# Causal grouped-query attention of a decoder's first layer, rewritten

## The chip, the cores and the metric

One core of one Trainium2 chip runs the whole program: four decoder layers over 1024 tokens of width 128. The metric is the device time of the program in microseconds (us). A core has five engines that work side by side and meet only at semaphores: TensorE (PE, matrix products, with its weight loads PEld), VectorE (DVE), ScalarE (ACT), GpSimd (POOL) and SyncE (SP, transfers). TensorE's clock has two levels, 1.2 and 2.4 GHz; a profile gives the granted clock as 0.50 or 1.00.

## The reference

The change lies in the first sublayer, x = x + attention(layernorm(x)):

```python
q = rms_norm(bitlinear(x, Wq).reshape(8, 128, 16, 8)...)   # in effect 1024 tokens, 16 heads of width 8
k = rms_norm(bitlinear(x, Wk)...)                          # 4 key and value heads
v = bitlinear(x, Wv)...
q, k = apply_rotary(q, cos, sin), apply_rotary(k, cos, sin)
q = q * q_gain[None, :, None, None]
k, v = jnp.repeat(k, 4, axis=1), jnp.repeat(v, 4, axis=1)
...                                                        # causal softmax(q k' / sqrt(8)) v
return bitlinear(y, Wp)
```

There are 1024 tokens, so eight tiles of 128. Each of 16 heads has a causal 1024 by 1024 matrix of scores; four heads share a key head. `bitlinear` rounds weights to three values and activations to 8 bits. The other eleven sublayers (cross-attentions, feed-forward layers, a scan and so on) are not touched.

## The kernel before

`ternary_attention` (L2095) normalises x, builds the quantised weights, projects to q, keys and values, turns them by the rotary table (L2216 to L2234), repeats keys and values for all 16 heads (L2236 to L2241), calls `attend` (L1021), and then projects and adds the result (L2243 to L2263). All this runs in blocks, one after the other, with a barrier of all engines at the end of each.

Before the weights are summed, VectorE writes `mask8` (L2135 to L2141): for each tile of queries a row of bytes over all 1024 keys, 251 where the key is later than the query and 0 elsewhere.

`attend` goes through the heads in eight pairs; a head of the pair is a = 0 or 1. Scores are exact to float32 by splitting queries and keys into three bf16 parts each and laying six products of parts below one another: `kstack` and `qstack` have 64 columns a head, of which 48 hold parts, one a constant, and three the shift. TensorE turns both stacks (L1191, L1197), and VectorE copies them to `kturned` and `qturned` (L1322, L1324), where head 0 has rows 0 to 51 and head 1 rows 64 to 115. GpSimd builds the next pair's stacks during the pair before (`stacks`, L1154).

For every pair, twice the scores are formed:
- Pieces ("chunk" items): TensorE multiplies a tile of queries with up to 512 keys (L1205), first all 12 of head 0 and then all 12 of head 1, and VectorE takes the row maxima under the byte mask with one fused instruction (L1334). From the maxima it computes the shift of each query, splits it into three parts and writes these into `qstack` (`place_shift`, L1351 to L1368). Then the queries are turned a second time.
- Scores: for a tile of keys t and a head a, TensorE forms the scores of all queries from 128 t on, in two products of up to 512 columns (L1225), and adds the mask of the diagonal block by a product of `mask8` with a diagonal matrix (L1229). ScalarE takes the exponential of up to 1024 columns at once (L1303). TensorE multiplies it, in float32, with the values and a column of ones (`weigh`, L1247): four products, for two heads and two halves of the queries, that lie on separate quarters of the array's columns, nine columns wide each.

Pieces of the next pair are put between the scores of this one, three places a tile (`some_items`), and go through a ring of three PSUM banks; scores have four banks and the weighed values one. At a pair's end ScalarE copies the four sums (L1309), TensorE turns them, and VectorE divides by the ones' sum and writes the output (L1340, L1342). The order is the same on each engine, and each waits for counts.

The kernel's own cross-attentions (`cross`, L1639, with the order from `programme`, L1610) already work by halves of the queries: pieces of both heads at once into two banks (L1762) with one reduction for both (L1885), scores of 512 columns (L1800), exponentials (L1855), weighings of two tiles of keys at once (L1816) and a fold of the sums (L1827).

Of the kernel before, what the change touches and what calls it, by code (L numbers as in the profile page):

```python
# [12 lines left out]
P = 128  # L13
T = 1024
NT = T // P
D = 128
H = 16
HD = D // H
# [1002 lines left out]
def attend(k, tiles, q, keys, values, out, key_mask=None, mask8=None, causal=False):  # L1021

    nc = k.nc
    n_keys = tiles * P
    kgroups = [range(a, min(a + 8, tiles)) for a in range(0, tiles, 8)]
    chunks = [(a, min(a + BANK, n_keys)) for a in range(0, n_keys, BANK)]
    NC, NG = len(chunks), len(kgroups)  # L1040

    def span(t, c):

        lo, hi = chunks[c]
        return lo, min(hi, (t + 1) * P) if causal else hi

    def first_query(t):

        return t * P if causal else 0


    prepare = ([("keys", g) for g in range(NG)] + [("queries", 0)] +
               [("chunk", a, t, c) for a in range(2) for t in range(NT) for c in range(NC) if span(t, c)[1] > span(t, c)[0]] +
               [("queries", 1)])
    G = len(prepare)
    FILL = 3 * (tiles - (4 if tiles > 2 * NT else 1))
    STEPS = 6 + (4 if mask8 is not None else 0)

    def before(p, a, b):

        if isinstance(p, int) and p == 0:
            return a
        return 2 * a + (p - 1) * (a + b)

    def items_of(p, par):

        first, last = isinstance(p, int) and p == 0, isinstance(p, int) and p == PAIRS - 1
        items = [] if last else [(item, p + 1, 1 - par) for item in prepare]
        return items if first else items[:NG] + [(("sums",), p - 1, 1 - par)] + items[NG:]

    def sums_place(p):
        return 0 if isinstance(p, int) and p == PAIRS - 1 else NG

    def phases(eng, phase, straight=False):

        phase(0, 0)
        if straight:
            for p in range(1, PAIRS):  # L1080
                phase(p, p % 2)
            return
        with eng.Fori(0, PAIRS // 2 - 1) as i:
            phase(2 * i + 1, 1)
            phase(2 * i + 2, 0)
        phase(PAIRS - 1, 1)

    with Stage(nc) as s:
        kstack = s.sb("kstack", [P, tiles, 2, SLOT], BF16)
        qstack = s.sb("qstack", [P, 2, NT, 2, SLOT], BF16)  # L1090
        kturned = s.sb("kturned", [P, 2, n_keys], BF16)
        qturned = s.sb("qturned", [P, 2, T], BF16)
        vstack = s.sb("vstack", [P, 2, tiles, 2, HD + 1])
        left = s.sb("left", [P, max(tiles, NT), 2, HD])
        probs = s.sb("probs", [P, 4, T])
        maxima = s.sb("maxima", [P, 2 * NT, NC])
        shift = s.sb("shift", [P, 2 * NT])
        shift_left = s.sb("shift_left", [P, 2 * NT])
        empty = s.sb("empty", [P, 2, 2 * NT])
        sums = s.sb("sums", [P, BANK])  # L1100
        inverse = s.sb("inverse", [P, 2 * NT])
        junk = s.sb("junk", [P, 4, BANK], BF16)
        cleared = s.sem("cleared")
        first_order = s.sem("first_order")
        no_maxima = s.sem("no_maxima")
        pool_order = s.sem("pool_order")
        stacks_ready = s.sem("stacks_ready")
        values_ready = s.sem("values_ready")
        ring_filled = s.sem("ring_filled")
        ring_free = s.sem("ring_free")  # L1110
        dve_order = s.sem("dve_order")
        shift_ready = s.sem("shift_ready")
        scores_filled = s.sem("scores_filled")
        probs_ready = s.sem("probs_ready")
        unit_done = s.sem("unit_done")
        sums_taken = s.sem("sums_taken")
        block = s.block()

        def ring(j):
            return 5 + j % 3  # L1120

        def score_buffer(n):
            return k.ps[:, 2 * (n % 2):2 * (n % 2) + 2, :].rearrange("p a b -> p (a b)")

        N_CLEAR = 6 + (key_mask is not None)

        def split(e, o, src, stack, first, second, third, last_step=None):

            rest = left[:, 0:src.shape[1]]

            def slot(i):
                return stack[:, :, :, i * HD:(i + 1) * HD]
            o.step(e.tensor_copy(slot(first[0]), src))
            o.step(e.tensor_tensor(rest, src, slot(first[0]), ALU.subtract))
            o.step(e.tensor_copy(slot(second[0]), rest))
            o.step(e.tensor_tensor(rest, rest, slot(second[0]), ALU.subtract))
            o.step(e.tensor_copy(slot(third[0]), rest))
            copies = [(slot(i), slot(part[0])) for part in (first, second, third) for i in part[1:]]
            for dst, src2 in copies[:-1]:
                o.step(e.tensor_copy(dst, src2))  # L1140
            return copies[-1]

        per_pair = 2 * 8 - 1

        def stacks(eng, e, o, pp, par):

            src = keys[:, :, 16 * pp:16 * pp + 16].rearrange("p t (a d) -> p t a d", a=2)
            dst, last = split(e, o, src, kstack, (0, 1, 2), (3, 4), (5,))
            o.step(e.tensor_copy(dst, last))
            src = q[:, :, 16 * pp:16 * pp + 16].rearrange("p t (a d) -> p t a d", a=2)  # L1150
            dst, last = split(e, o, src, qstack[:, par], (0, 3, 5), (1, 4), (2,))
            e.tensor_copy(dst, last).then_inc(stacks_ready, 1)
            eng.wait_ge(stacks_ready, pp + 1)


        @block.gpsimd
        def _(pool):
            pool.wait_ge(cleared, N_CLEAR)

            def value_stack(pp, par):  # L1160
                src = values[:, :, 16 * pp:16 * pp + 16].rearrange("p t (a d) -> p t a d", a=2)
                nc.gpsimd.tensor_copy(vstack[:, par, :, :, 0:HD], src).then_inc(values_ready, 1)

            def stacks_of(pp):
                stacks(pool, nc.gpsimd, InOrder(pool, pool_order, (pp - 1) * per_pair), pp, pp % 2)

            value_stack(0, 0)
            value_stack(1, 1)
            pool.wait_ge(ring_filled, NG)
            pool.wait_ge(stacks_ready, 1)  # L1170
            stacks_of(1)
            for pp in range(2, PAIRS):

                pool.wait_ge(ring_filled, before(pp - 2, G, 1) + NG)
                stacks_of(pp)
                pool.wait_ge(unit_done, (pp - 1) * tiles)
                value_stack(pp, pp % 2)


        @block.tensor  # L1180
        def _(pe):
# [2541 lines left out]
```

## Time and profile before

| | us |
|---|---|
| median of 3 runs | 6687.87 (6675.5 to 6690.6) |
| the profiled execution | 6692.29 |
| its span, first to last instruction | 6690.5 |
| `attend`, first clear to last output | 73.1 to 407.0 |
| TensorE busy in the span | 4558.4 (68%) |
| VectorE, ScalarE, GpSimd busy | 3719.9, 2700.4, 753.0 |

Mean granted clock of TensorE over the span: 0.79. A row of the windows gives a stretch, its length, each engine's busy time with the number of instructions, the granted clock, the share of time in which the DMA engines worked, and GB/s. A row of the timeline gives start, duration, engine, line, operation, output<-inputs, shape out<-in and how many instructions it merges; for a matmul the shape begins with rows*columns of its weights.

### The profile page before, as it was taken

How to read it: one execution, taken by the hardware profiler on the slowest of the kernel's cores; microseconds unless marked ns; L12 is line 12 of the kernel's file. 1: busy time of each engine (PE TensorE's matmuls, PEld its weight loads, DVE VectorE, ACT ScalarE, POOL GpSimd, SP SyncE). 2: the span in 40 equal slices, each digit the busy share in tenths (PEclk: the TensorE clock that was granted, in tenths of full speed). 3: DMA queues.
4: the chain of work that ended last, by engine and by line, in shares of the span. 5: the costliest groups of instructions: out<-in, count | busy, mean ns of one | idle time of the engine just before them, and what ended most of it. 6: DMA issues, size and time to landing. Idle time of an engine off the chain costs nothing. (4 is left out here: it accounts for less than half of the span.)

```text
span 6690.5 us, 85981 instructions
## 1 busy us (share of the span) xinstructions
PE 4558.4 (68%) x32752; PEld 1806.1 (27%) x32752; DVE 3719.9 (56%) x8303; ACT 2700.4 (40%) x4930; POOL 753.0 (11%) x949
## 2 busy tenths in 40 slices
PE   5866999533799999999737999997764040524326
PEld 1233444322122222222431222222443030313225
DVE  5444666555877777774349989894343030412314
ACT  1322666233366666666214777787101010101103
POOL 1100000001000000000020000000002627161350
PEclk5567999767799999999867999999865555555557
DMA  0020000033000000000030010000040000000000
GB/s 12 0 48 18 10 14 9 14 146 106 1 11 11 11 11 10 3 10 1 6 96 1 11 22 11 11 11 10 24 130 5 11 4 12 2 11 4 7 10 3
DMA packets 105806, 142.42 MB, mean 21 GB/s; under 512 B 41998, under 2 KB 82029, under 8 KB 102512
## 3 DMA queue, kind: packets, MB, share of 16 engines
q1 hardware_dynamic: 65742, 118.14, 6.7%
q0 software_dynamic: 20480, 10.53, 1.0%
q10 hardware_dynamic: 19178, 8.34, 0.5%
q8 instruction: 255, 4.18, 0.3%
q14 instruction: 151, 1.24, 0.1%
HBM read 103.79 MB, written 33.14 MB: 20 GB/s over the span
## 5 line engine op out<-in xcount | busy, mean ns | idle before, releaser
L1855 ACT ACTIVATE probs<-ps 128x512 f32<-128x512 f32 x3264 | 1734.3, 598 | 762.8 <-PE ps L1800 762.6
L1890 DVE CUSTOM_DVE_ANT_0 junk<-ps,mask 128x512 bf16<-128x512 f32 (+1 forms) x1664 | 1049.2, 678 | 380.1 <-PE ps L1762 364.0
L1885 DVE TENSOR_REDUCE maxima<-ps 128x2 f32<-128x1024 f32 (+1 forms) x832 | 956.6, 1200 | 128.2 <-PE ps L1762 121.9
L1816 PE MATMUL ps<-probs,vstack 128*9 128x512 f32 x6528 | 872.6, 596 | 0.4 <-ACT probs L1855 0.4
L1800 PE MATMUL ps<-qturned,kturned 52*128 52x512 bf16 x3264 | 793.4, 386 | 83.5 <-ACT probs L1855 64.5
L1762 PE MATMUL ps<-kturned,qturned 49*128 49x512 bf16 (+1 forms) x3328 | 704.6, 392 | 139.4 <-DMA kturned<-ends_row 56.3
L3189 POOL DMA_INDIRECT line<-table,index x640 | 609.5, 952 | 1204.9 <-DVE index L3460 580.5
L1793 PE MATMUL ps<-maskT,lower 128*128 128x512 fp8e5 x1632 | 562.5, 387 | 63.6 <-ACT probs L1855 15.1
L1800 PEld LDWEIGHTS ps<-qturned,kturned 52*128 52x128 bf16 x3264 | 196.2, 93 | 791.8 <-ACT probs L1855 462.1
L1762 PEld LDWEIGHTS ps<-kturned,qturned 49*128 49x128 bf16 x3328 | 166.3, 95 | 520.9 <-issue 234.5
L3513 DVE SCALAR_TENSOR_TENSOR x_sb<-ps,gate,x_sb 128x128 f32<-128x128 f32 x64 | 22.5, 351 | 499.4 <-DMA rows<-in_ctx 349.7
L1793 PEld LDWEIGHTS ps<-maskT,lower 128*128 128x128 bf16 x1632 | 123.5, 96 | 599.1 <-ACT probs L1855 434.0
L3289 PE MATMUL ps<-hash_b,ones 1*128 1x128 f32 x128 | 37.3, 378 | 345.5 <-issue 293.5
L3346 ACT ACTIVATE hash_hid<-ps,hash_b 128x128 f32<-128x128 f32 x256 | 73.1, 369 | 475.0 <-DMA rows<-in_ctx 318.8
L2775 PE MATMUL ps<-plane,bands 32*32 32x512 f32 x6720 | 249.6, 608 | 17.6 <-DVE top L2927 17.6
L2873 ACT COPY powerT<-ps 128x512 f32<-128x512 f32 x280 | 164.2, 586 | 203.5 <-PE ps L2789 203.4
L2917 DVE SCALAR_TENSOR_TENSOR plane<-keep,ps 128x1024 f32<-128x1024 uint8 x144 | 175.7, 1220 | 102.7 <-PE ps L2757 102.3
L2865 ACT ACTIVATE power<-power,bias 128x512 f32<-128x512 f32 x280 | 202.5, 724 | 56.1 <-DVE bias L2935 56.1
L1544 POOL MEMSET vall<- 128x816 f32 x2 | 3.1, 1567 | 1872.2 <-POOLq L66 1872.2
L2789 PE MATMUL ps<-ident,power 128*128 128x128 f32 x1120 | 183.0, 286 | 32.4 <-ACT powerT L2873 31.4
L2927 DVE CUSTOM_DVE_ANT_0 power<-ps,lose 128x512 f32<-128x512 f32 x280 | 176.9, 687 | 41.5 <-PE ps L2775 41.5
L3319 ACT ACTIVATE dev_h<-red 128x16 f32<-128x16 f32 x16 | 3.4, 215 | 423.4 <-issue 261.3
(731 smaller groups left out, 5569.0 us busy)
## 6 DMA issues: line engine op xcount, KB each, us to landing
raw<-in_mask_BxSxS_if SPq DMA_DIRECT2D x8, 3202.0 KB, 13.2
kturned<-keys_parts SPq DMA_DIRECT2D x192, 102.0 KB
table<-lines SPq DMA_DIRECT2D x51, 256.0 KB, 2.3
line<-table,index POOLq DMA_INDIRECT x640
keys_parts<-parts SPq DMA_DIRECT2D x24, 384.0 KB, 2.5
values_heads<-vall SPq DMA_DIRECT2D x2, 3672.0 KB, 10.7
vstack<-values_heads SPq DMA_DIRECT2D x16, 459.0 KB, 16.8
lose<-in_mask_SxS_bc SPq DMA_DIRECT2D x32, 128.0 KB
```

The source lines that it names most:

```text
L1762: last = nc.tensor.matmul(ring(e)[:, a * BANK:a * BANK + hi - lo], qturned[rows, par, t * P:(t + 1) * P], kturned[rows, par, lo:hi], start ...
L1793: nc.tensor.matmul(k.ps[:, (v + j) % 3, :], k.lower[:], maskT[:, t, b * BANK:(b + 1) * BANK], start=True, stop=False, skip_group_check=True)
L1800: nc.tensor.matmul(k.ps[:, v % 3, :], kturned[rows, par, t * P:(t + 1) * P], qturned[rows, par, b * BANK:(b + 1) * BANK], start=maskT is N ...
L1816: last = nc.tensor.matmul(k.ps[at:at + HD + 1, 3, :], vstack[:, p % 2, a, t, :], probs[:, (h * KT + t) % slots, a, :], start=(t < 2), stop ...
L1855: nc.scalar.activation(probs[:, u % slots, a, :], k.ps[:, (2 * u + a) % 3, :], ACT.Exp, scale=(1.0 if maskT is None else 1.0 / STEP8)).the ...
L1885: nc.vector.tensor_reduce(dst, ring(e).rearrange("p (a n) -> p a n", a=2)[:, :, 0:hi - lo], AX.X, ALU.max).then_inc(ring_free[at % 2], 1)
L1890: nc.vector.tensor_tensor_reduce(junk[:, at % 2, a * BANK:a * BANK + hi - lo], ring(e)[:, a * BANK:a * BANK + hi - lo], mask8[:, 4 * b + m ...
L2775: last = nc.tensor.matmul(k.ps[32 * j:32 * j + 32, i, :], bands[32 * i:32 * i + 32, 4 * g + j, c, :], plane[32 * i:32 * i + 32, u % 2, j, ...
L2789: last = nc.tensor.transpose(k.ps[:, 6, m * P:(m + 1) * P], power[:, u % 2, i, (4 * b + m) * P:(4 * b + m + 1) * P], k.ident[:])
L2865: nc.scalar.activation(part, part, ACT.Exp, bias=bias[:, u % 2, 1, i:i + 1], scale=1.0 / TINY).then_inc(powers, 1)
L2927: nc.vector.tensor_tensor_reduce(power[:, u % 2, i, b * BANK:(b + 1) * BANK], k.ps[:, i, :], lose[:, win % 2, i, b * BANK:(b + 1) * BANK], ...
L3189: nc.gpsimd.indirect_dma_start(line[:, t % 4, j, :], None, lines_of, bass.IndirectOffsetOnAxis(ap=index[:, t, j:j + 1], axis=0)).then_inc( ...
```

## The change

`attend` is replaced by `causal_attend`, with an order of its own:
- The stacks of all 8 pairs (queries) and all 4 key heads are built at once at the start, on VectorE and ScalarE (queries) and GpSimd (keys and values), and kept. Keys and values are no longer repeated. The keys of a key head are turned once for its two pairs.
- The work goes by halves of the queries: 16 halves h (pair h // 2, b = h % 2), with 4 tiles of keys for b = 0 and 8 for b = 1. One exponential covers one head's 512 queries at most; scores have three PSUM banks, the weighed values one, and the ring two pairs of banks.
- A piece holds both heads: two products into two banks. VectorE takes both maxima with one reduction, without a mask. Instead TensorE adds a constant to the diagonal block by a further product per head. Bytes and `mask8` go; `hidden` is one 128 by 128 block.
- The pieces of half h + 2 are spread over the units of half h; the shift of half h + 1 stands second in that queue. `weigh` takes two tiles of keys for both heads.

```diff
+def causal_programme(lag):
+    def chunks_of(h):
+        return [("piece", h, m, c) for m in range(4) for c in range(h % 2 + 1)]
+    queue = []
+    for h in range(HALVES):
+        mine = chunks_of(h + 2) if h + 2 < HALVES else []
+        if h % 2 == 0 and h + 2 < HALVES:
+            p = (h + 2) // 2
+            mine = ([("keys", p // 2)] if p % 2 == 0 else []) + [("queries", p)] + mine
+        if h and h + 1 < HALVES:
+            mine.insert(1, ("shifted", h + 1))
+        queue.append(mine)
+    queue[0] = chunks_of(1) + [queue[0][0], ("shifted", 1)] + queue[0][1:]
+    out = [("keys", 0), ("queries", 0)] + chunks_of(0) + [("shifted", 0)]
...
+            late.setdefault(u + lag, []).append(("weigh", h, t // 2))
...
+        cut = [-(-len(queue[h]) * (3 * t + j) // (3 * n)) for j in range(4)]
+        out += [("score", h, t, 0)] + queue[h][cut[0]:cut[1]] + [("score", h, t, 1)] + queue[h][cut[1]:cut[2]]
+        out += late.pop(u, []) + queue[h][cut[2]:cut[3]]
...
+        def _(pool):
+            o.step(nc.gpsimd.tensor_copy(k_slot(0, 0), src))
...
+            nc.gpsimd.tensor_copy(kstack[:, :, :, 1, 0:half].rearrange("p t v r -> p (t v) r"),
+                                  kstack[:, :, :, 0, 0:half].rearrange("p t v r -> p (t v) r")).then_inc(keys_ready, 1)
...
+            def piece(e):
...
+                for a in range(2):
+                    rows = slice(a * SLOT, a * SLOT + SHIFT)
+                    last = nc.tensor.matmul(ring(e)[:, a * BANK:a * BANK + n], qturned[rows, p, t * P:(t + 1) * P],
+                                            kturned[rows, p // 2, c * BANK:c * BANK + n], start=True, stop=not at_end,
+                                            skip_group_check=True)
+                if at_end:
+                    for a in range(2):
+                        last = nc.tensor.matmul(ring(e)[:, a * BANK + n - P:a * BANK + n], k.lower[:], hidden[:], start=False, stop=True,
+                                                skip_group_check=True)
...
+            def score(e):
...
+                masked = [m for m in range(4) if m == t - 4 * b or (b, t, m) == (0, 1, 0)]
+                last = nc.tensor.matmul(k.ps[:, v % 3, q0:], kturned[rows, p // 2, t * P:(t + 1) * P],
+                                        qturned[rows, p, b * BANK + q0:(b + 1) * BANK], start=True, stop=not masked,
+                                        skip_group_check=True)
...
+            def weigh(e):
...
+                for t in (2 * i, 2 * i + 1):
+                    q0 = first_column(b, t)
+                    for a in range(2):
+                        at = 32 * (2 * a + t % 2)
+                        last = nc.tensor.matmul(k.ps[at:at + HD + 1, 3, q0:], vstack[:, p // 2, t, :],
+                                                probs[:, unit_at[h, t] % slots, a, q0:],
+                                                start=(t < 2), stop=(t >= n - 2), skip_group_check=True)
...
+                nc.vector.tensor_reduce(dst, ring(e).rearrange("p (a n) -> p a n", a=2)[:, :, 0:n], AX.X,
+                                        ALU.max).then_inc(ring_free[ring_at[e] % 2], 1)
```

`first_column(b, t)` is 128 times the tiles by which t lies inside the half, and 0 for the second tile of the first half, whose first block is masked whole.

## Rows read from the trace of the kernel before

**Rows 1.** windows of 138 to 403 and 3580 to 3660 us, all engines
```profile
core 0: us, PE busy (x) PEld busy (x) DVE busy (x) ACT busy (x) POOL busy (x), PEclk, DMA share, GB/s
138.00:378.00 240.00, 210.89 (x840) 53.28 (x838) 106.46 (x384) 76.53 (x122) 27.99 (x86) 0.50 0.00 0
...
378.00:403.00 25.00, 23.39 (x86) 5.10 (x86) 0.71 (x3) 11.56 (x20) 0.00 (x0) 0.50 0.00 1
...
3580.00:3585.00 5.00, 4.75 (x22) 0.83 (x20) 3.61 (x4) 3.03 (x7) 0.00 (x0) 0.60 0.01 3
3600.00:3660.00 60.00, 54.96 (x377) 12.51 (x375) 53.35 (x54) 48.06 (x93) 2.62 (x8) 1.00 0.00 1
```

**Rows 2.** waits between 138 and 378 us: engine, line <- released by: us, times, longest
```profile
PE ps L1197 <- DVE qstack L1368: 18.6, 6, 3.1
...
PE ps L1210 <- ACT sums L1309: 9.5, 6, 1.6
```

**Rows 3.** timeline of ScalarE in the stage, copies of the sums
```profile
137.94 2.38 ACT L1309 COPY sums<-ps 9x512 f32<-9x512 f32 x4 [7.92 <-PE ps L1247]
...
377.04 2.38 ACT L1309 COPY sums<-ps 9x512 f32<-9x512 f32 x4 [8.00 <-PE ps L1247]
...
403.00 2.38 ACT L1309 COPY sums<-ps 9x512 f32<-9x512 f32 x4 [1.12 <-PE ps L1247]
```

**Rows 4.** timeline of VectorE, first mask byte and what follows the last
```profile
26.12 0.23 DVE L2139 TENSOR_SCALAR mask<-later 128x128 uint8<-128x128 f32 x1 [0.36 <-DVE total L2134]
...
34.63 1.22 DVE L2143 TENSOR_REDUCE total<-rows 128x1 f32<-128x128 f32 x4
```

**Rows 5.** timeline, first repeated copy, and the stage's first clears
```profile
69.82 0.29 DVE L2240 COPY keys<-turn 128x256 f32<-128x256 f32 x1
...
73.10 0.48 DVE L1370 MEMSET kstack<- 128x512 uint32 x1 [0.69 <-PEq L66]
73.74 0.91 DVE L1371 MEMSET qstack<- 128x1024 uint32 x1 [0.16 <-issue]
```

**Rows 6.** timeline, TensorE's first transposes of the stage
```profile
80.16 1.04 PE L1191 MATMUL ps<-ident,kstack 128*128 128x128 bf16 x8 [28.34 <-DVE qstack L1152]
```

**Rows 7.** the page's groups: line engine op, shapes xcount | busy, mean ns | idle
```profile
L1885 DVE TENSOR_REDUCE maxima<-ps 128x2 f32<-128x1024 f32 (+1 forms) x832 | 956.6, 1200 | 128.2 <-PE ps L1762 121.9
```

**Rows 8.** groups of GpSimd by shape: xcount | busy us, mean ns | idle
```profile
L1550 POOL CAST parts<-rest 128x512 bf16<-128x512 f32 x24 | 22.9, 954 | 1.5
L1133 POOL CAST kstack<-keys 128x128 bf16<-128x128 f32 x7 | 2.1, 296 | 22.3 <-PE ps L1191 22.3
```

**Rows 9.** timeline of TensorE in the last pair
```profile
392.43 0.60 PE L1225 MATMUL ps<-qturned,kturned 52*128 52x512 bf16 x1
392.97 0.29 PE L1229 MATMUL ps<-lower,mask 128*128 128x128 bf16 x1
393.19 1.90 PE L1247 MATMUL ps<-probs,vstack 128*9 128x128 f32 x8
395.02 0.50 PE L1225 MATMUL ps<-qturned,kturned 52*128 52x384 bf16 x1
...
398.14 0.39 PE L1225 MATMUL ps<-qturned,kturned 52*128 52x256 bf16 x1
...
398.68 0.39 PE L1225 MATMUL ps<-qturned,kturned 52*128 52x256 bf16 x1
...
399.23 1.46 PE L1247 MATMUL ps<-probs,vstack 128*9 128x384 f32 x4
400.62 0.28 PE L1225 MATMUL ps<-qturned,kturned 52*128 52x128 bf16 x1
```

**Rows 10.** timeline of TensorE in the third layer's cross-attention, just started
```profile
3579.16 0.61 PE L1762 MATMUL ps<-kturned,qturned 49*128 49x512 bf16 x2
3579.57 0.73 PE L1800 MATMUL ps<-qturned,kturned 52*128 52x512 bf16 x2
```

**Rows 11.** timeline, the step after the stage
```profile
407.30 1.22 DVE L2076 TENSOR_REDUCE scale<-out 128x8 f32<-128x1024 f32 x1 [0.34 <-PEq L66]
```

More of the change, by code:

```diff
@@ L2058, in cross_attention, with tiles_of, first_column @@
         project_add(k, k.hT, wo[:], bias[:, 2, :])
+KV_HEADS = 4
+def tiles_of(b):
+    return 4 * b + 4
+def first_column(b, t):
+    if (b, t) == (0, 1):
+        return 0
+    return max(t - 4 * b, 0) * P
+def causal_programme(lag):
[12 more added lines that the diff above has]
+    out = [("keys", 0), ("queries", 0)] + chunks_of(0) + [("shifted", 0)]
+    units = [(h, t) for h in range(HALVES) for t in range(tiles_of(h % 2))]
+    late = {}
+    for u, (h, t) in enumerate(units):
+        if t % 2:
+            late.setdefault(u + lag, []).append(("weigh", h, t // 2))
+        if t == tiles_of(h % 2) - 1:
+            late.setdefault(u + lag + 2, []).append(("sums", h))
+    for u, (h, t) in enumerate(units):
+        n = tiles_of(h % 2)
+        cut = [-(-len(queue[h]) * (3 * t + j) // (3 * n)) for j in range(4)]
+        out += [("score", h, t, 0)] + queue[h][cut[0]:cut[1]] + [("score", h, t, 1)] + queue[h][cut[1]:cut[2]]
+        out += late.pop(u, []) + queue[h][cut[2]:cut[3]]
+    for u in sorted(late):
+        out += late[u]
+    return out
@@ L2109, in ternary_attention @@
         table = s.sb("table", [P, 2, NT, HD // 2])
-        mask8 = s.sb("mask8", [P, NT, T], FP8)
+        later = s.sb("later", [P, P])
         intT = s.sb("intT", [P, T], BF16)
         q = s.sb("q", [P, NT, D])
-        keys = s.sb("keys", [P, NT, D])
-        values = s.sb("values", [P, NT, D])
+        keys = s.sb("keys", [P, NT, KVD])
+        values = s.sb("values", [P, NT, KVD])
         out = s.sb("out", [P, NT, D])
@@ L2117, in ternary_attention @@
             rows = g.sb("rows", [P, 4, D])
-            later = g.sb("later", [P, P])
             total = g.sb("total", [P, 4])
@@ L2234, in _ @@
                 o.step(nc.vector.tensor_copy(q[:], turn1[:, :, 0:D]))
[L2236 to L2242 removed]
+                o.step(nc.vector.tensor_copy(keys[:], turn1[:, :, D:D + KVD]))
+                o.step(nc.vector.tensor_copy(values[:], small[:, :, KVD:2 * KVD]))
+        causal_attend(k, q, keys, values, later, out)
         quantise(k, out, intT, scale)
```

571 lines of the change are left out of this document (245 added, 326 removed).

## The prediction, written before the changed kernel had run

> **What bounds the kernel now.** I read first the windows of the first layer's attention [rows 1]: from 138 to 378 us TensorE is busy 210.9 of 240.0 us, VectorE 106.5, ScalarE 76.5, and the granted clock is 0.50, the lower level (1.2 GHz). So TensorE bounds this stage; VectorE and ScalarE have more than half of their time free. Then the waits of the same stretch [rows 2]: TensorE itself stands for 18.6 us in six places for the shift that VectorE has put into the query stack, and for 9.5 us in six for ScalarE's copy of the sums: 28.1 of the 29.1 us in which it was not busy, 4.7 us a pair of heads. Then the sums' copies on ScalarE, which mark the pairs [rows 3]: eight of them, six equal periods of 39.85 us between 137.94 and 377.04 us, and 25.96 us for the last pair, which has no pieces to prepare beside it. The stage is 334 us (73.1 to 407.3), 5% of the span; nothing outside it is touched but what stands right before it.
>
> **The change, part by part**, for the profiled execution, whose 6692.3 us (span 6690.5) lie 4.4 us above the median of the runs.
>
> Ahead of the stage. The mask bytes go: VectorE built them with nothing beside it from 26.12 to 34.63 us [rows 4]. Minus 8.5 us. The eight repeated copies of keys and values, 0.33 us apart, become two of a quarter of a full tile: 2.6 us become about 0.8, minus 1.8 [rows 5]. Being on VectorE alone, both are full gains.
>
> The start. Before, the stage clears two stacks, splits one pair, and TensorE starts 7.1 us after it [rows 5, 6]. Now VectorE splits all queries (three casts and two subtractions of 1024 elements, about 1.2 us at most each [rows 7]: 5 us) while GpSimd splits the keys, fills the head's second half and copies four value slices. GpSimd takes 0.30 us for 128 elements and 0.95 for 512 [rows 8]; so six copies of 256 are 2.7 us, two subtractions 1.3, the copy of 1536 elements 2.5 (bounds 1.0, were it one more small one, and 2.9, three times 0.95), four small ones 0.8, with gaps 7.7. It starts after two clears (0.48 and 0.91 us [rows 5]). TensorE then starts at 73.1 - 8.5 - 1.8 + 1.4 + 7.7 = 72 us instead of 80.2.
> The Trainium skill (Advanced Engine Details and Errata, VectorE Performance Modes) says that GpSimd and VectorE block each other where VectorE works in a two-port mode. If GpSimd had to wait for VectorE's 5 us, TensorE would start at 77; no row here shows that, and the sum doesn't use it.
>
> TensorE per pair at the lower clock, from start to start in the last pair of before, where it never waits [rows 9]. A score of 512 columns takes 0.54 with the change to the mask's full-height product, the mask 0.22 with the change back: 0.76; without a mask 0.43. With 256 columns and mask 0.54; so 384 is 0.65 and 128 is 0.44. A weighing of four products side by side takes 1.83 when the longest has 512 columns, 1.38 at 384 (so 0.95 at 256, 0.5 at 128).
> - Weighings: before, 5 x 1.83 + 1.38 + 0.95 + 0.5 = 12.0. Now two tiles of keys are weighed at once, four times at 512 and twice at 256 columns: 4 x 1.83 + 2 x 0.95 = 9.2.
> - Scores: the first half of the queries 2 x (0.76 + 0.87 + 0.54 + 0.44) = 5.2 (the second tile runs all 512 columns with two masks: 0.87), the second half 8 x 0.43 + 2 x (0.76 + 0.65 + 0.54 + 0.44) = 8.2. Sum 13.4, 0.5 to 1 more than before.
> - Pieces: both heads' products lie on different rows of the array and run side by side: two of them at 512 columns cost 0.41 [rows 10], so 4608 columns cost 3.9, where two heads one after the other cost 7.7. But each of the 8 diagonal pieces now gets two masks on TensorE (VectorE masked them before): 2 x 0.11 plus 0.22 for changing over and back, 3.5. Sum 7.4: what running in pairs saves, the masks nearly eat.
> - Transposes: 20 instead of 24, eight cost 1.04 [rows 6]: 2.6. Sums: two small folds at 0.6 or less each: 1.2.
> Together 33.8. Where a score without mask runs beside a piece of the other head, something is saved (1); I take 33.0 (bounds 31 and 36). The 4.7 us of waiting a pair go, since shifts are wanted two halves after their pieces began and the sums' copy lies under the next units' scores; what comes next is ScalarE, busy 12.8 us a pair before and about as much now plus the transposes' copies, and VectorE with 12 reductions of at most 1.2 us and the shifts: both under 20 us. So 39.85 becomes 33.0 in the steady pairs. The fold's end costs 2 us where the old one cost 4.3 [rows 3, 11], and the first half's pieces, which nothing covers, about 4 of waiting: from TensorE's start 8 x 33 + 4 + 2 = 270 us, end at 342 instead of 407.3: minus 65 us.
>
> The clock. The stage of before stays at 0.50 even from 378 to 403 us, where TensorE is busy 23.4 of 25 us [rows 1]. What it did there: scores on 52 of 128 rows one at a time, between masks and weighings. The unmasked attention of the third layer, which runs pieces of both heads in pairs as this change does, comes to the higher level (2.4 GHz) in 3580 to 3585 us after pairs and one weighing without a pause, and stays at 1.00 [rows 1, 10]. The new stage lies between: pairs, but shorter columns and about 60 changes of array layout a pair. Were it at 1.00 throughout, the 60 changes of 0.11 us would stay (6.6), the other 26.4 halve (13.2), and about 3 of waits for VectorE's shift and ScalarE would show: 23 a pair, 184 + 11 = 195 us. I expect it to rise in the dense stretches and fall again: three tenths of the way from 270 to 195, 247 us, end at 319, minus 88. I choose three tenths because most of a half (masked scores of one head) resembles the stage that never rose, and only the start of each second half resembles the one that did.
> The Trainium skill (TensorE: Matmul & The Clock Gate, Why this matters for your kernels) gives the full clock to a TensorE that is kept busy without a pause; the 23.4 of 25 us at 0.50 disagree, so that rule alone is no reason to expect it, and it is one of the rivals.
>
> Sum: 6692.3 - 88 = 6604; against the runs, 6600 us.
>
> **The rivals.**
> - Lower clock throughout: minus 65, 6623. For it: [rows 1] at 403 us. Against: pairs, and fewer waits.
> - Higher clock nearly throughout: 73.1 to 407.3 shrinks by 140, 6548. For it: [rows 1] at 3600 us. Against: 128-column scores with masks. It is also what the Trainium skill's rule above would give.
> - New waits at each half: the shift's chain (maximum, three casts, transposes, copy) comes later than the score that wants it, 3.1 us as the six of before [rows 2], for 16 halves: 50 us given back, 6650. For it: the queue of the first half of a pair has four tiles only. Against: it is placed second in the queue, after a whole half.
> - Slower: the ring has two buffers, and TensorE issues in order. If each of the 96 pieces held TensorE for a whole reduction of 1.2 us [rows 7], 115 us would be added to the 6600: 6715. It decides from 0.92 us a piece on. Against: VectorE would have to be the bound, and it is busy 14 of 33 us.
> - The pairing does nothing (the products of both heads don't run side by side, or masks cost double): 28 us back, 6628.
>
> **How the numbers follow.** Forecast 6600: 0.50. Lower clock or no pairing: 0.27. Higher clock: 0.08. New waits: 0.10. Slower: 0.03. Other waits that just cancel it: 0.02. What this kernel can tell from no change is about 0.2%, 13 us. Faster 0.95, same 0.02, slower 0.03. The range for 8 in 10: 6576 (three fifths of the way to the higher clock, or 2 us a pair less than counted) to 6630 (the lower clock and 1 us a pair more).
>
> **What would show it.** Attention's last output at 319 us from the span's start (342 at 0.50, 267 at 1.00); mean clock there 0.6 to 0.7; pairs 33 us apart where the clock is 0.50 and 23 where it is 1.00; TensorE's first transpose at 72 us; no wait of TensorE over 1 us for the shift; diagonal pieces 0.4 us longer than the others. It is wrong if GpSimd's copy takes over 4 us, if TensorE waits for reductions in every piece, or if later stages move by more than 10 us.

## The result, and the profile after

The changed kernel takes 6638.5 us (median of 10 runs, 6601.4 to 6663.3) against 6691.8 us before (median of 10, 6675.5 to 6732.0): ratio 0.9909, 95% interval 0.988 to 0.9937, 53 us less. The forecast was 6600, its range ended at 6630. The direction was right; the gain was forecast 38 us too large. The same kernel on another chip gave 6613.8 (six runs, ratio 0.9885, 0.9852 to 0.9919), so two sets of runs, on two chips, differ by more than the 8.5 us to the range's edge.

The profiled run after has 6630.0 us (span 6628.1), 62.3 less than the one before. (Its mean granted clock reads 0.809, but the first 197 us of that count as 1.00 and were not, as shown below.) First the timeline ahead of the stage (start, us, engine, line):

```profile
25.87 0.06 DVE L2094 MEMSET total<- 128x4 f32 x1 [0.89 <-PEq L66]
26.30 0.90 DVE L2096 TENSOR_REDUCE total<-rows 128x1 f32<-128x128 f32 x3 [0.36 <-DVE total L2094]
...
62.90 0.91 DVE L1996 MEMSET qstack<- 128x1024 uint32 x1 [0.80 <-PEq L66]
...
64.27 0.63 DVE L1999 CAST qstack<-q 128x1024 bf16<-128x1024 f32 x1
...
65.24 1.52 POOL L1802 TENSOR_TENSOR k_left<-keys,kstack 128x256 f32<-128x256 f32 x1
...
66.26 1.05 DVE L2002 CAST qstack<-q_left 128x1024 bf16<-128x1024 f32 x1
...
71.42 1.47 POOL L1810 COPY kstack<-kstack 128x1536 bf16<-128x1536 bf16 x1
...
73.74 1.01 PE L1820 MATMUL ps<-ident,kstack 128*128 128x128 bf16 x8 [30.26 <-POOL vstack L1813]
```

The reductions start at 26.30 where the first mask byte was [rows 4], the stage's clears at 62.90 where they were at 73.10 [rows 5]: 10.2 us, as counted. TensorE starts at 73.74 (forecast 72, before 80.16 [rows 6]).

Then TensorE in the stage. Steady stretch, and places that answer to the forecast's prices:

```profile
142.31 0.61 PE L1837 MATMUL ps<-kturned,qturned 49*128 49x512 bf16 x2
142.71 0.64 PE L1857 MATMUL ps<-qturned,kturned 52*128 52x512 bf16 x2
...
205.29 1.86 PE L1889 MATMUL ps<-fold,sums 128*128 128x18 f32 x8 [0.44 <-DVE maxima L1979]
207.09 1.90 PE L1879 MATMUL ps<-probs,vstack 128*9 128x512 f32 x8
208.91 0.61 PE L1820 MATMUL ps<-ident,qstack 128*128 128x128 bf16 x4
...
214.01 1.06 PE L1889 MATMUL ps<-fold,sums 128*128 128x18 f32 x8
215.00 1.04 PE L1879 MATMUL ps<-probs,vstack 128*9 128x512 f32 x8
...
259.83 1.03 PE L1879 MATMUL ps<-probs,vstack 128*9 128x256 f32 x8
260.80 0.50 PE L1837 MATMUL ps<-kturned,qturned 49*128 49x384 bf16 x2
```

From start to start: two pieces of 512 columns, one of each head, 0.40; a weighing of four 512-column products 1.82 and of four 256-column products 0.97 at the lower clock. These are the forecast's 0.41, 1.83 and 0.95. The fold of the sums is not: 1.80 at the lower clock (205.29 to 207.09) and 0.99 at the higher (214.01), where the forecast had "0.6 or less each".

Windows (columns as in [rows 1]), and ScalarE's copies of the sums, one a half:

```profile
142.00:177.00 35.00, 34.56 (x164) 11.70 (x162) 14.21 (x28) 14.62 (x30) 0.00 (x0) 1.00 0.00 0
240.00:280.00 40.00, 39.12 (x185) 13.61 (x184) 14.82 (x31) 15.86 (x31) 0.00 (x0) 0.50 0.00 1
214.00:228.00 14.00, 14.00 (x110) 6.02 (x108) 8.03 (x15) 8.43 (x19) 0.00 (x0) 1.00 0.01 2
```

```profile
131.52 0.58 ACT L1954 COPY sums<-ps 128x512 f32<-128x512 f32 x1 [0.62 <-PE ps L1879]
142.46 0.58 ACT L1954 COPY sums<-ps 128x512 f32<-128x512 f32 x1 [0.23 <-PE ps L1879]
166.54 0.58 ACT L1954 COPY sums<-ps 128x512 f32<-128x512 f32 x1 [0.62 <-PE ps L1879]
177.48 0.58 ACT L1954 COPY sums<-ps 128x512 f32<-128x512 f32 x1 [0.23 <-PE ps L1879]
...
212.02 0.62 ACT L1954 COPY sums<-ps 128x512 f32<-128x512 f32 x1
226.51 0.58 ACT L1954 COPY sums<-ps 128x512 f32<-128x512 f32 x1 [0.20 <-PE ps L1879]
```

One more spacing, of an odd half in which keys are turned as well:

```profile
235.42 0.58 ACT L1954 COPY sums<-ps 128x512 f32<-128x512 f32 x1 [0.23 <-PE ps L1879]
260.94 0.58 ACT L1954 COPY sums<-ps 128x512 f32<-128x512 f32 x1 [0.62 <-PE ps L1879]
```

The step after the stage, on VectorE:

```profile
340.71 1.22 DVE L2037 TENSOR_REDUCE scale<-out 128x8 f32<-128x1024 f32 x1 [0.33 <-PEq L66]
```

Two things are to be seen. (A half with four tiles of keys is called even below, one with eight odd; a pair is one of each.) First, from 142 to 177 us the window reads 1.00 for the clock, yet the 512-column products there take 0.61 us as in the stretch at 0.50; at 1.00 they take 0.39. The column holds 1.00 until the first recorded change of level, at 197 us here, and the durations decide. By them 26 of the 112 scores of 512 columns in the stage ran at the higher clock (2.4 GHz). Second, the spacings: wholly at the lower clock an even half takes 10.9 us and an odd one 24.1, 35.0 a pair (before 39.85 [rows 3], forecast 33.0); an odd half wholly at the higher clock takes 14.5. The forecast's 33.0 was a mean over pairs with and without a turning of keys. Three of the odd spacings hold such a turning (eight transposes more, and two short waits); the two of them wholly at the lower clock take 25.5, 36.5 a pair, so the mean to hold against 33.0 is 35.6. The stage ends at 340.71 (before 407.30 [rows 11], forecast 319): 66.6 us less. The rest of the program, the same code, took 6287.4 us after that point against 6283.2: 4.2 of the 66.6 were given back there.

TensorE's waits between 84 and 341 us (us in total, times, longest):

```profile
PE ps L1889 <- DVE maxima L1979: 3.4, 6, 0.8
PE ps L1820 <- DVE qstack L1970: 3.2, 4, 1.9
```

Both are small beside the 18.6 and 9.5 us in 240 of [rows 2]: those waits went, and no new one of that size took their place.

### The profile page after: what moved, and what is told of

Read it like the earlier page. It is cut to its first block and busy times, and to the rows that moved or that the text cites. A ratio compares the mean times of both kernels' runs of the same rounds, so it can differ in the third digit from the quotient of the medians.

```text
span 6628.1 us, 85529 instructions
## 1 busy us (share of the span) xinstructions
PE 4530.1 (68%) x32960; PEld 1824.6 (28%) x32960; DVE 3683.5 (56%) x7977; ACT 2720.7 (41%) x5009; POOL 720.7 (11%) x842
```

## The experiments

Where the clock matters, each kernel is read by three numbers of its profile: spacings of halves in which no, or every, 512-column score took 0.39 us; the count of such scores among all of 512 columns; and where the stage ends. A few scores lie across a change of level, so a count is good to about 2. Most kernels have one profile; the kernel after has three, the one with transposes two. The rest of the program varied from 6277 to 6321 us between profiles of the same code on the chips where the kernel before takes 6690 us, so totals of one run say less than the stage.

**The fold as transposes.** In `add_up`, and one reduction on VectorE adds the parities:

```
-    last = nc.tensor.matmul(ring(e)[:, m * 32:...], sums[:, h % 2, m * P:...], fold[:], ...)
+    last = nc.tensor.transpose(ring(e)[:, m * P:...], sums[:, h % 2, m * P:...], k.ident[:])
```

> The sums' fold, four products of a full 128x128 f32 stationary against 18 columns (two passes each, 1.85 us for the four at the lower clock, 16 times in the stage; counted as 0.6 in the prediction), becomes four f32 transposes as the kernel before had (1.11 us for four at the lower clock), and VectorE adds the two tile parities with one small reduction. Theory 1 (the fold is the term that was mis-sized, and TensorE sets the pace): a low-clock pair goes from 35.0 to 33.5 us, the stage loses 12 us, total about 6627, with the same share of the higher clock. Theory 2 (the miss is the clock's share and the fold's length is covered by something else that ends as late, such as the reductions of the pieces): the low-clock pair stays within 0.3 us of 35.0 and the total does not move. VectorE's added 0.2 us a half should cost nothing in either.

6586.6 us (4 runs), ratio 0.9841 (0.9805 to 0.9876). The stage ends at 295.5 us, 45 earlier, and 74 scores of 112 ran at the higher clock. An even half at the lower clock takes 10.2 in place of 10.9, which is the fold's shorter length, so theory 2, that the length is covered, falls. Theory 1 is right on the length, but 52 us less than the first runs of the kernel after are four times what it gives. That asked for the clock's part. Theory 3: long weight loads with few columns hold the clock down.

**No masks on the pieces.** The two `hidden` products of `piece` go.

> The two mask products on each of the 8 diagonal pieces of a pair are left out, so the row maximum is taken over the hidden half of the diagonal block too. That is still a shift common to the row, so the softmax is the same up to rounding. The prediction priced these masks and the changes of array layout around them at 3.5 us a pair. If that holds, a low-clock pair goes from 35.0 to 31.5 us and the total falls by 28, to about 6610; more if TensorE's clock rises more often without them. Rival: the pieces' ring is what paces the stage (VectorE's reductions), so that masks hide in its waits; then the pair stays at 35.

6620.2 us (4 runs), ratio 0.989 (0.9852 to 0.9929). Halves at the lower clock take 10.2 and 21.9 us, 32.1 a pair: 2.9 less, where 3.5 was counted. Stage end 328.2; 30 scores of 112.

**Both pieces on the same rows**, and **one half ahead**:

```
-    rows = slice(a * SLOT, a * SLOT + SHIFT)       # piece
+    rows = slice(0, SHIFT)
```
```
-        mine = chunks_of(h + 2) if h + 2 < HALVES else []
+        mine = chunks_of(h + 1) if h + 1 < HALVES else []
...
+            mine.append(("shifted", h + 1))
```

> The second head's piece uses the rows of the first head (its shift is then the first head's, all else is the same work). Two products on the same rows can't run side by side. If the pairing of heads gives what the prediction counted (3.9 us a pair), a low-clock pair goes from 35.0 to 38.9 us and the total is 31 us more, about 6670. If the products never ran side by side, nothing changes. The trace should show two 512-column pieces 0.43 us apart at the lower clock in place of nearly together.

11.4 and 26.4 us, 37.8 a pair: pairing is worth 2.8, not 3.9. Part of the 3.9 is kept, since a piece also runs beside a score of the other head; here a piece and a score start together:

```profile
213.16 0.60 PE L1837 MATMUL ps<-kturned,qturned 49*128 49x512 bf16 x1
213.17 0.61 PE L1857 MATMUL ps<-qturned,kturned 52*128 52x512 bf16 x1
```

Stage end 355.7, 15 later (34 of 112 scores at the higher clock gave part back); total of one run 6645.3.

> Pieces are prepared one half ahead in place of two, and the shift of a half is put in at the end of the half before it. If having the shift two halves ahead is what took the waits away, TensorE waits for VectorE's shift chain at each of 15 halves, about 3 us each as in the kernel before, and some more for reductions since the 8 pieces of an odd half now lie in the short half: 45 to 60 us more, about 6690. If the waits of before came from elsewhere, less than 10 us.

One run, 6664.7 us, stage end 371.9, 31 later. TensorE's waits between 84 and 371 us:

```profile
PE ps L1819 <- DVE qstack L1969: 21.3, 9, 3.0
```

So having the pieces two halves ahead, with the shift at the start of the next queue and not at its end, is what took away the waits of [rows 2]; the edit moves both, and which of the two does more is not shown. The waits for the shift are 18 us more than in the kernel after, since a wait shows at only 9 of 15 halves; those for ScalarE's copy behind the shift went from 0.7 to 6.1. The rest of the 31 us goes with fewer scores at the higher clock (22 of 112).

**Scores side by side.** Both heads' scores back to back, then their masks:

```
-        out += [("score", h, t, 0)] + queue[h][cut[0]:cut[1]] + [("score", h, t, 1)] + queue[h][cut[1]:cut[2]]
+        out += [("score", h, t, 0), ("score", h, t, 1)] + queue[h][cut[0]:cut[2]]
```

> The scores of both heads of a key tile are issued one right after the other (different rows of the array, different banks), then their masks; the fold stays as it is. In the kernel after, they are apart, with pieces between. Side by side they save 1408 + 3328 columns a pair, 3.9 us at the lower clock, and 8 changes of layout of 0.11 us on the masked tiles: 4.8 us less what some scores saved already by running beside a piece (0.8): a low-clock pair goes from 35.0 to about 31, the total by 32, to 6606, with the clock's share as it is. If what keeps the clock down is the fold, the share of 512-column scores at the higher clock stays near the 26 of 112 of the kernel after. If it is single scores on half of the rows, the share rises to over half, and the total falls below 6590. Rival on the other side: three score banks are too few for pairs, TensorE waits for ScalarE's exponentials at each unit, and the pair stays at 35.

6614.8 us (4 runs), ratio 0.9893 (0.9857 to 0.9929), stage end 322.2, 36 of 112 scores, where over half was expected if single scores hold the clock down. An even half takes 10.6; no steady odd half stayed at the lower clock throughout, so the pair was not measured.

**Fold twice, fold in bfloat16, fold in bfloat16 with 128 columns.** These take theory 3 apart.

> Each fold is done twice (same result), 16 products in place of 8 records of it. If its cost is only its own length, 1.85 us at the lower clock and 1.05 at the higher, the total is 25 to 30 us more, 6665, and the share of scores at the higher clock stays near 26 of 112. If the fold is what holds the clock down (theory 3, formed after the run with transposes, where 74 of 112 of the 512-column scores took 0.39 us in place of 26), the share falls towards none and the total is near 6685 to 6690.

One run, 6682.7; 12.6 and 25.8 us, 38.4 a pair: 3.4 more, twice the fold's length. But 40 of 112 scores ran at the higher clock, where theory 3 asked for about none.

> Sums and fold matrix are rounded to bfloat16, so the four folds are 4 short products of 18 columns, with 0.1 us of weights each: about 0.5 us in place of 1.85 at the lower clock. The result of the stage is rounded to 8 bits here, all else is computed as before. Theory 1 (only the length counts): pair at the lower clock 35.0 - 2.7 = 32.3 us, total 6638 - 21 = 6617, share of the higher clock 26 of 112. Theory 3 (the 1.85 us of weight loads with few columns hold the clock down; gone, it rises as with transposes): share about 74 of 112, total about 6575. If narrow products by themselves hold it down, however short, it is 6617 too, so that 6575 would speak for the length of the loads.

6624.2 us (6 runs), ratio 0.991 (0.988 to 0.9939):

```profile
241.06 0.59 ACT L1957 CAST sums<-ps 128x512 bf16<-128x512 f32 x1 [0.62 <-PE ps L1880]
250.82 0.59 ACT L1957 CAST sums<-ps 128x512 bf16<-128x512 f32 x1 [0.23 <-PE ps L1880]
273.29 0.59 ACT L1957 CAST sums<-ps 128x512 bf16<-128x512 f32 x1 [0.62 <-PE ps L1880]
```

9.8 and 22.5 us are 32.2 to 32.3 a pair, 2.7 less, what the fold's length was expected to give. The fold itself takes 0.21 us from start to start:

```profile
254.23 0.28 PE L1890 MATMUL ps<-fold,sums 128*128 128x18 bf16 x4
254.44 1.90 PE L1880 MATMUL ps<-probs,vstack 128*9 128x512 f32 x8
```

The stage ends at 324.0. 33 of 112 scores at the higher clock: the long loads went, and the count was far from the 74 that theory 3 asked for. Theory 3 falls with these two; theory 1 stands at the lower clock.

> The bfloat16 fold with its moving matrix padded with zeros from 18 to 128 columns: the four products take as long or 0.1 us longer than the narrow ones, nothing else changes, and sums are rounded to 8 bits as there. The fold as transposes (128 columns each) ran 74 of 112 scores at the higher clock, the narrow bfloat16 fold 33, the narrow f32 fold 26. Theory 4 (a transpose keeps columns moving behind the weighings, a narrow product does not): here the share is as with transposes, 60 or more, the total near 6580. Theory 5 (the width does not matter and the 74 came from something else of that run, or by chance of where the clock's rises fell): the share stays at 25 to 40, the total at the 6624 of the narrow bfloat16 fold.

This run, the next two and the last one below (transposes with scores side by side and all masks) were on a chip on which the kernel before takes 6004.1 us; only ratios and the stage compare. Ratio 0.9826 (0.9798 to 0.9855), stage end 303.4, 57 of 112 scores: between what theory 4 and theory 5 asked for, and read beside the next run.

**The kernel after once more, and weighing tile by tile** (`at = 64 * a`, so that two products run side by side and not four):

> The kernel after, once more, profiled again: how far the share of the higher clock (26 of 112), the end of the stage (340.7 us) and what the rest of the program takes (6287.4 us from there to the end) move from one execution to the next of the same kernel. The rest has been 6277 to 6321 us in the eight runs so far, all with the same code there. If the share is a matter of chance it differs by 15 or more here; the pairs at the lower clock have to be 35.0 us again.

Ratio 0.9873 (0.9838 to 0.9907), 86 us less than before there. Again 35.0 a pair at the lower clock (10.9 and 24.1), but 57 of 112 scores at the higher, stage end 311.8: 29 us earlier than in the first profile. The wide fold had the same 57, so nothing shows that the width of a fold in bfloat16 sets the clock; its 8 us in the stage are no more than its shorter length gives (an even half at the lower clock 9.8 in place of 10.9, an odd one at the higher 13.8 in place of 14.5). The higher level is reached at other places in each profile of the same kernel, and this alone moves the stage by tens of us. The profiles are from three chips, so chip and chance are not told apart.

> Key tiles are weighed one at a time, two products (both heads) side by side on two groups of columns in place of four. A weighing of four 512-column products took 1.8 us. If side by side is what makes two tiles cost as much as one, each tile takes these 1.8 us by itself, and a low-clock pair goes from 35.0 to 44 us, the total by 70 us to about 6710. If the products never ran side by side, nothing changes.

5926.2 us in one run, 8 more than the median of the kernel after there, not 70. The stage ended at 332.3, 20 later than in the profile of the kernel after on the same chip; the rest of that run was 9 us shorter. TensorE at about 205 us, at the higher clock:

```profile
205.03 1.89 PE L1879 MATMUL ps<-probs,vstack 128*9 128x512 f32 x8
```

The weighing did double (1.89 against 1.04 at 215.00 above), so four do run side by side. But 94 of 112 scores ran at the higher clock; odd halves took 18.8 there. The lengthened work is 70 us at the lower clock and some 38 at the higher (18.8 and 8.7 a pair of halves against 14.5 and 8.3), and the stage was only 20 us longer, with more of it at the higher level. From this comes a wider form of theory 4, tested next: work added to TensorE can go with a higher clock and so cost little.

**All on one chip: before, after, fold as transposes, and a filler.** The filler adds work that nobody reads:

```
+                for m in range(4):
+                    last = nc.tensor.matmul(ring(e)[:, BANK:2 * BANK], k.lower[:], kturned[:, 0, 0:BANK], start=True, stop=True)
```

> The kernel before once more, profiled on the chip that runs the other three: its stage is expected at 334 us (73.1 to 407.3) again, with pairs of 39.85 us and the lower clock throughout, since its stage never rose in the first profile. If its pairs come under 39 us here, the clock of this stage differs from chip to chip, or from run to run, for the kernel before as well.

It came out otherwise: the stage ends at 397.7, not 407.3, since one stretch (about 228 to 246 us) ran at the higher clock. Here from its profile:

```profile
140.00:220.00 80.00, 70.33 (x280) 17.81 (x280) 35.49 (x128) 25.48 (x42) 11.31 (x36) 0.50 0.00 1
228.00:246.00 18.00, 14.84 (x91) 4.37 (x89) 13.68 (x53) 6.00 (x12) 0.00 (x0) 0.92 0.00 0
```

> The kernel after, on one chip with the others of this call. The share of 512-column scores at the higher clock was 26 of 112 in one profile and 57 in another, the stage ended at 340.7 and 311.8 us. If that is chance, it falls anywhere between here; if it belongs to the chip, it is near one of these two, and the ratio to the kernel before near 0.991 or 0.987 with it. Pairs at the lower clock 35.0 us.

6613.8 us (6 runs), 75 less than before; 46 of 112, stage end 324.2; a whole pair at the higher clock took 14.5 + 8.3 = 22.8.

> The fold as f32 transposes once more, beside the kernel after on the same chip. By its length alone it saves 12 us at the lower clock and 6 to 7 at the higher (1.05 us become 0.63): the difference of the two medians is 7 to 12 us. If transposes also raise the clock (74 of 112 scores against 26 or 57), the difference is 20 to 50 us; over the first chip's runs it was 52 us.

6595.7 us (6 runs), ratio 0.9863 (0.9835 to 0.9892): 18 less than the kernel after, between the 7 to 12 of the length and the 20 to 50 of length and clock. The runs of the two overlap (6576.8 to 6620.6 and 6595.7 to 6658.9), so the totals don't decide. In the profiles the stage ends at 294.3, 30 earlier, again with 74 of 112. The fold itself, at either clock:

```profile
135.67 1.11 PE L1890 MATMUL ps<-ident,sums 128*128 128x128 f32 x4
...
177.09 0.63 PE L1890 MATMUL ps<-ident,sums 128*128 128x128 f32 x4 [0.84 <-DVE maxima L1979]
```

This is 0.7 and 0.4 shorter than the products, 12 us in 16 at the lower clock. At the higher it is less than 7: an odd half takes 14.1 in place of 14.5, an even one 8.3 in both. The other 20 us or so of these two profiles are the clock's.

> Behind each fold of the kernel after, four products of 128 rows and 512 columns are added that nobody reads (the other bank of the fold's own ring buffer): 16 times 1.7 us at the lower clock or 0.85 at the higher, 14 to 27 us of work more. If the clock does not care, the total is 14 to 27 us over that of the kernel after in this call. If products with many columns behind the fold raise the clock (theory 4; weighing tile by tile doubled the weighings' columns and ran 94 of 112 scores at the higher clock, for only 20 us more in the stage), the share is over 70 of 112, and the total is within 10 us of the kernel after, or below it.

6608.8 us (4 runs), ratio 0.9884 (0.9854 to 0.9914), stage end 307.6, 91 of 112. Its filler, beside the fold:

```profile
139.69 1.06 PE L1889 MATMUL ps<-fold,sums 128*128 128x18 f32 x8
140.60 1.02 PE L1892 MATMUL ps<-kturned,lower 128*128 128x512 bf16 x4
```

The 16 fillers are about 19 us of useless work (from start to start most take 0.95, five 1.80), and the stage is 17 us shorter than that of the kernel after on the same chip. That is less than the 29 us by which the kernel after moves by itself, so the shortening is not shown to be the filler's; the count of 91, like the 94 of weighing tile by tile, is far outside the 26 to 57 of its three profiles. The totals (6608.8 and 6613.8) can't be told apart, and so are within the 10 us that theory 4 asked for. And the stretch from 139 to 239 us in the three profiles on this chip (after, transposes, filler):

```profile
139.00:239.00 100.00, 95.62 (x595) 36.23 (x594) 50.57 (x99) 52.55 (x107) 0.00 (x0) 0.76 0.00 1
```
```profile
139.00:239.00 100.00, 91.84 (x656) 34.34 (x655) 60.64 (x122) 59.34 (x123) 0.00 (x0) 0.91 0.00 1
```
```profile
139.00:239.00 100.00, 92.28 (x661) 38.13 (x662) 54.55 (x108) 53.80 (x111) 0.00 (x0) 0.94 0.00 1
```

The kernel with the busiest TensorE (95.6, in part because it runs slower) has the lowest clock (0.76) of the three.

**Versions that beat both.** Transposed fold, scores side by side, and either no masks on the pieces and a later wait for the values, or all masks:

> All that helped at once: the fold as transposes, no masks on the pieces (the shift is then taken over the hidden half of the diagonal block too; same softmax up to rounding), both heads' scores side by side, and the wait for the value copies moved to the first weighing. At the lower clock a pair is 35.0 - 1.5 - 4.0 - 4 = 25.5 us: 8 pairs are 204 and with start and end the stage ends near 290 even without any higher clock. With the share of the kernel with the transposed fold (two thirds) it ends near 265, the total about 6542. If VectorE (15 us a pair) or ScalarE (15 us a pair and its waits) becomes the bound, TensorE waits show and the pair stays over 22 us also at the higher clock, total about 6560.

6571.8 us (5 runs), ratio 0.9817 (0.9794 to 0.9839), stage end 282.2, 56 of 112; the expected 6542 was missed since the clock rose less, while the pair at the higher clock took 12.8 + 7.9 = 20.7.

> The fold as f32 transposes and both heads' scores side by side, with every mask kept: the same computation as the kernel after. At the lower clock a pair is 35.0 - 1.5 - 4.5 (what scores side by side gave: the two shortest steady spacings of that run sum to 31) = 29.5 us. If the masks' columns help the clock (56 of 112 scores at the higher clock without them on the pieces, 74 with them), the share is again about 74 of 112, the stage ends near 280 us and the total is about 6565, as good as the kernel that leaves the pieces' masks out (6572). If the shares of 56 and 74 are only chance, it is 5 to 10 us slower than that one, about 6580.

Ratio 0.9809 (0.978 to 0.9839; the kernel after there 0.9873), stage end 287.2, 72 of 112; the pair at the higher clock took 21.4. The masks cost 0.7 us a pair there, and both versions are equal within what these runs tell. Either takes 0.6 to 0.9% off the kernel after, ratio against ratio.

## Why the prediction was right or wrong

- **Ahead of the stage: right.** 10.2 us against 10.3. GpSimd's big copy took 1.47 us (bounds 1.0 to 2.9, taken 2.5), but its subtractions 1.52 each and not 0.65, and VectorE's later casts 1.05 where its first took 0.63. TensorE started 1.7 us late. The Trainium skill (GPSIMD Engine Reference, Specifications) names contention between the two engines where VectorE has two operands in SBUF. The rows agree as far as GpSimd's subtractions beside VectorE's are long; they don't show 5 us in which GpSimd stands still, and no run took the two engines apart.
- **Waits that go: right.** 4.7 us a pair before; the stage after has 3.4 and 3.2 us in all, about 10 with the small ones. That the order of pieces and shifts did it was shown by moving them back.
- **The failed step: "Sums: two small folds at 0.6 or less each: 1.2".** A fold takes 1.80 us at the lower clock, 1.2 more. 16 x 1.2 = 19 us. That its length is paid in full was shown by the bfloat16 fold, which gives back 2.7 us a pair, and by folding twice, which costs 3.4. The prediction named no row for its 0.6; these rows of the kernel before bear on it (the old fold, four transposes, from TensorE's timeline; then the third layer's fold from the groups by shape between 3600 and 4800 us: times, busy us, mean ns, idle):

```profile
140.37 1.11 PE L1210 MATMUL ps<-ident,sums 128*128 128x128 f32 x4 [1.51 <-ACT sums L1309]
...
405.52 0.63 PE L1210 MATMUL ps<-ident,sums 128*128 128x128 f32 x4 [2.57 <-ACT sums L1309]
```
```profile
L1827 PE MATMUL ps<-fold,sums 128*128 128x18 f32 x128 | 16.7, 263 | 2.9 <-ACT sums L1870 0.7 <-DVE maxima L1885 0.6
```

 The old fold took 0.63 only at the stage's very end, where the clock was up already, and 1.11 at the lower level. And the very products of the change stood in that trace, in the third layer: 16.7 us for 16 folds, 1.04 each at the higher clock, so that 0.6 was no bound at all. With 1.8 the forecast's pair is 33.0 + 2.4 = 35.4, and the mean measured is 35.6 (35.0, or 36.5 where keys are turned). The Trainium skill (FP8 and Floating Point Precision, TensorE Precision Notes) gives a float32 product four passes; the trace shows two records for each product of the fold and one for each transpose, so it agrees that the product is dear (1.80 against 0.21 for the bfloat16 fold), and doesn't show four passes.
- **Prices that nearly cancel.** Masks on pieces cost 2.9 a pair (counted 3.5), and pairing of pieces saves 2.8 (counted 3.9, of which the score beside it was left open). That four weighings run side by side was right.
- **The clock: size right in this profile, by luck.** With every shortened half put back to 24.1 (25.5 where keys are turned) and 10.9 us, the stage would have ended at about 366, an estimate from the spacings. It ended at 340.7, so the clock gave some 26; the forecast had 23 (342 to 319). Two more profiles of the same kernel gave 42 and 55. The price at the higher clock came out, 22.8 a pair against 23, though the fold in it took 0.97 to 0.99. In the forecast's sum for 1.00 throughout, the 11 us outside the pairs (184 + 11) have no working; with the 4 + 2 of the other sum it is 190, and the forecast moves by under 2 us.
- **The account.** For the profiled execution 6604 was forecast and 6630.0 measured, 26 more. 22 of them lie in the stage (end 340.7, forecast 319): 19 from the folds, 2 from the later start, some 4 that the small waits about cover (3.4 of them before folds), less the 3 that the clock gave beyond its 23. 4 lie in the rest of the program. From there to the medians, 6600 and 6638.5, it is 12 more: the profiled run after lay 8.5 below its median, and the forecast had taken off the 4 by which the profiled run before lay above its own. Without the 19 us of the folds the median would be about 6620, inside the range.
- **The signs it named.** No wait for the shift over 1 us: one of 1.9. Later stages within 10 us: 4.2. Diagonal pieces 0.4 us longer: 0.33 (143.49 to 143.82). Mean clock in the stage 0.6 to 0.7: about 0.60, if all before 197 us is taken at 0.50 as the durations say. Attention's end at 319, or 342 at 0.50: 340.7, which looked like the second and was a dearer fold with the clock's gain on top.
- **Rivals.** Lower clock throughout would have been about 6656 in the profiled run (stage end 366), not 6623; new waits, the ring's 1.2 us a piece and useless pairing didn't happen. Of the Trainium skill's rule (TensorE: Matmul & The Clock Gate, Why this matters for your kernels), that a TensorE kept busy gets the full clock: at 240 to 280 us it was busy 39.1 of 40 us at 0.50. The rule alone fails here.

What stays open is what raises the clock. Float32 transposes of the sums went with 74, 74 and 72 of 112 scores at the higher clock, but with 56 in the version without masks on the pieces, and a bfloat16 fold of 128 columns, shorter still, with 57. Adding work went with 91 (products of 512 columns) and 94 (weighing tile by tile), but with 40 where the fold was done twice. Each of these counts is of one profile, beside a kernel whose own count moved from 26 to 57 over three chips. That a busy TensorE alone doesn't bring the higher level is shown; a rule for when it comes was not established.

## What to carry to other kernels

Read a small operation's price at the clock at which it will run, and look through the whole trace for the same operation and type: the row with 16.7 us for 16 folds was there. In a stage in which TensorE's clock moves, a change is to be judged by spacings that lie wholly at one level and by several profiles, since the same kernel ended its stage at 340.7, 324.2 and 311.8 us. Where the clock moves, an operation's length may not be its price: with the fold replaced the stage was 30 and 45 us shorter for 12 us of length at most, and 19 us of added work did not show in the total.

## What the runs showed of the hardware that was not expected

- Weighing with two products side by side in place of four, twice the time on TensorE, added 20 us to the stage in place of 70, and 19 us of useless products added nothing that shows: 94 and 91 of 112 scores ran at the higher clock against 57 and 46 on the same chips.
- TensorE busy for 39.1 of 40 us stayed at 0.50 (240 to 280 us of the kernel after).
- The kernel before, whose stage stayed at 0.50 in one profile, had one stretch at the higher clock in another, worth 9.6 us.
- At the lower clock four float32 products with 18 columns and 128 columns of weights each take 1.80 us from start to start, four transposes of the same data 1.04, four bfloat16 products of 18 columns 0.21.
- A GpSimd subtraction of 256 float32 elements beside a VectorE subtraction of 1024 took 1.52 us. Of VectorE's three casts of 1024 elements, all beside GpSimd, the first took 0.63 us and the later two 1.05; why is not shown.
